# The sums of the log decays: one sequence's high and low parts stacked on the partitions, two levels at once

## What is computed

```
x_in, z = split(rmsnorm(x) @ in_proj_w)            # 512 channels each
x_in  = silu(x_in)
a_mod = sigmoid(x_in @ A_proj_w + A_proj_b)        # a decay for each token and channel
B, C  = x_in @ B_proj_w, x_in @ C_proj_w           # 16 states
for t in tokens:                                   # within one sequence
    h   = a_mod[t] * sigmoid(A_base) * h + B[t] * x_in[t]
    y[t] = sum over states of h * C[t]
out = x + ((y + D * x_in) * silu(z)) @ out_proj_w
```

## Time and profile before

| | |
|---|---|
| median of three runs | 1854.79 us |
| the runs | 1848.14, 1854.79, 1855.22 us |
| span of the profiled execution | 1852.3 us |
| busy: matmuls / weight loads | 1661.7 us / 1285.1 us |
| busy: VectorE / ScalarE / GpSimd | 1149.3 / 918.0 / 849.6 us |
| one iteration in the middle | 52.44 us |

### The profile page before, as it was taken

The page is one execution under the profiler, slowest core; times in us unless marked ns, Lnnn a source line. Parts: engine busy times, 40 slices in busy tenths (PEclk is TensorE's granted clock), DMA queues, the critical chain, the costliest instruction groups (busy, mean ns, idle before and its releaser), DMA issues.

```text
span 1852.3 us, 38642 instructions
## 1 busy us (share of the span) xinstructions
PE 1661.7 (90%) x11791; PEld 1285.1 (69%) x11791; DVE 1149.3 (62%) x2536; ACT 918.0 (50%) x2231; POOL 849.6 (46%) x552
## 2 busy tenths in 40 slices
PE   2248999999999999999999999999999999999775
PEld 2136777777777777777777777777777777777653
DVE  2465666666667666676666666666666666766432
ACT  0224555555554555555555555555545555555421
POOL 1024545555444455554444455554444555545431
PEclk9579999999999999999999999999999999999986
DMA  7110000000000000000000000000000000000000
GB/s 219 52 29 7 2 10 10 10 0 9 9 9 9 9 9 9 3 6 9 9 9 9 9 9 9 0 9 9 9 9 9 9 9 4 5 9 7 7 4 6
DMA packets 40234, 26.57 MB, mean 14 GB/s; under 512 B 19826, under 2 KB 38274, under 8 KB 40196
## 3 DMA queue, kind: packets, MB, share of 16 engines
q1 hardware_dynamic: 40196, 26.09, 5.4%
HBM read 21.37 MB, written 4.71 MB: 14 GB/s over the span
## 4 chain that ended last, share of the span: by engine, by line
PE 81%; DVE 8%; issue 5%; ACT 3%; SPq 2%; POOL 1%; DVEq 0%; DMA 0%; POOLq 0%; ACTq 0%
PE bank L742 13%; PE bank L679 13%; PE bank L707 7%; PE bank L819 6%; PE bank L633 6%; PE bank L635 5%; PE bank L634 5%; PE bank L734 4%; PE bank L720 4%; PE bank L808 3%; PE bank L834 3%; PE bank L663 2%; DVE a_sum L1264 2%; SPq L455 2%; PE bank L799 1%
## 5 line engine op out<-in xcount | busy, mean ns | idle before, releaser
L1624 POOL TENSOR_TENSOR y<-y,u 128x512 f32<-128x512 f32 x128 | 162.7, 1271 | 47.3 <-DVE u L1357 42.1
L1604 POOL TENSOR_TENSOR resid<-xres,a_c 128x256 f32<-128x256 f32 x32 | 23.3, 727 | 346.5 <-DVE x L1365 346.5
L1616 POOL TENSOR_TENSOR u<-xe,Ef 128x512 f32<-128x512 f32 x96 | 122.7, 1292 | 42.8 <-ACT Ef L1092 42.8
L679 PEld LDWEIGHTS bank<-a_xnT,a_wq 128*128 128x128 f32 x1024 | 126.8, 195 | 17.1 <-issue 14.1
L819 PE MATMUL bank<-u,Gm 128*128 128x512 f32 x256 | 130.1, 611 | 4.7 <-DVE Gm L1349 3.8
L633 PE MATMUL bank<-w_e_hi,cT_hi 128*128 128x512 f32 x256 | 122.5, 478 | 10.2 <-DVE c_c L1413 10.2
L679 PE MATMUL bank<-a_xnT,a_wq 128*128 128x128 f32 x1024 | 127.5, 279 | 0.0
L742 PEld LDWEIGHTS bank<-a_wo,a_prob 128*128 128x128 f32 x512 | 96.0, 192 | 43.9 <-ACT a_prob L995 31.8
L1585 POOL TENSOR_TENSOR a_prob<-a_prob,a_mask 128x1024 f32<-128x1024 f32 x32 | 75.6, 2363 | 109.0 <-DVE a_prob L1235 109.0
L679 PE MATMUL bank<-c_xnT,c_wq 128*128 128x128 f32 x1024 | 125.4, 282 | 0.0
L742 PE MATMUL bank<-a_wo,a_prob 128*128 128x256 f32 x512 | 120.0, 388 | 5.4 <-ACT a_prob L995 3.4
(11 more groups left out here) (294 smaller groups left out, 4427.5 us busy)
## 6 DMA issues: line engine op xcount, KB each, us to landing
a_xin<-in_x SPq DMA_DIRECT2D x32, 128.0 KB, 2.4
xres<-in_x SPq DMA_DIRECT2D x32, 128.0 KB, 2.6
out<-acc SPq DMA_DIRECT2D x32, 128.0 KB, 1.7
a_wq<-in_L_cond_Wq SPq DMA_DIRECT2D x1, 1024.0 KB, 5.4
a_wo<-in_L_cond_Wo SPq DMA_DIRECT2D x1, 1024.0 KB, 6.5
c_wq<-in_L_cond_Wq SPq DMA_DIRECT2D x1, 1024.0 KB
c_wo<-in_L_cond_Wout SPq DMA_DIRECT2D x1, 1024.0 KB
u<-in_L_ffn_expert_w SPq DMA_DIRECT2D x3, 256.0 KB, 4.0
```

The costliest lines, as they stand in the source:

```text
L679: mm = pe.matmul(bank(f"q{half}")[:, m * P:(m + 1) * P], X.wq[:, k, hp * P:(hp + 1) * P], X.xnT[:, k, :], start=k == 0, stop=k == KD - 1)
L1616: pool.tensor_tensor(u[l][:, :], xi[:, :], (E0u if l == 0 else Ef[l])[:, :], ALU.mult)\
L1624: pool.tensor_tensor(y[:, :], y[:, :], tm[l][:, :], ALU.add).then_inc(g.done(f"y{l}"), 1)
```

## The change

For each of the two sequences there is now one operand, `nl_stacked[b]` (named `nl_seq0` and `nl_seq1` in the rows), that has the high parts of the sequence's 64 tokens on one half of the partitions and the low parts on the other half. The matrix of two levels stands side by side in one 128x128 operand, its 64x64 block repeated for the two halves: one matmul sums high and low part over the contraction and gives two levels of one sequence, the first on partitions 0 to 63 of the bank, the second on 64 to 127. The four matmuls are E0 and E1 (levels 0 and 1, sequences 0 and 1) and E2 and E3 (levels 2 and 3).

- `log_a` writes the two high halves in two instructions of 64x512, waits for the second, and then takes the full logarithm as before. `nh` subtracts in two instructions of 64x512, each from one half of the partitions to the other.
- The exponentials come from banks that hold two levels of one sequence. Each is now 64x512, ten a tile in place of five. The step E0u is gone from `ORDER`; its two halves stand in E0 and E1. E0 and E1 have three exponentials each, E2 and E3 two each. Those whose level and sequence differ in number read one half of the partitions and write the other.
- The banks are freed by the last exponential that reads them. VectorE's and GpSimd's readers of a level wait for its second half.
- The table of sums and the buffer for it are half as wide.

```diff
@@ constants
-    parts["sums"] = np.concatenate(sums, 1)
+    stacked = [np.tile(a[0:S, 0:S], (2, 1)) for a in sums]
+    parts["sums"] = np.concatenate(stacked, 1)
@@ RESULTS
-"nl": "nh nl"
+"nl": "nh0 nh1 nl", "E0": "E0u0 E00 E10", "E1": "E0u1 E01 E11", "E2": "E20 E30", "E3": "E21 E31"
-"nh": "nl"
+"nh": "nl0 nl1"
@@ TURNS (which result frees the bank)
-b.E0@2>act.E0u   b.E1@2>act.E1    b.E2@2>act.E2    b.E3@2>act.E3
+b.E0@2>act.E10   b.E1@2>act.E11   b.E2@2>act.E30   b.E3@2>act.E31
@@ buffers
-        nl_parts = parts("nl", [P, E2])
+        nl_stacked = [sb(f"nl_seq{b}", [P, E2], F32R) for b in range(BT)]
@@ TensorE
-                def E(l):
+                def E(n):
+                    pair, b = n // BT, n % BT
+
                     def run(t):
-                        pe.wait_ge(*banks.free(f"b.E{l}", t))
-                        if l == 0:
-                            pe.wait_ge(*dve.at("nl", t))
-                        for n, part in enumerate(nl_parts):
-                            mm = pe.matmul(banks[f"b.E{l}"][:, :], sums[:, l * P:(l + 1) * P], part[:, :],
-                                           start=n == 0, stop=n == 1)
-                        mm.then_inc(p.done(f"E{l}"), 1)
+                        pe.wait_ge(*banks.free(f"b.E{n}", t))
+                        if n == 0:
+                            pe.wait_ge(*dve.at("nl1", t))
+                        pe.matmul(banks[f"b.E{n}"][:, :], sums[:, pair * P:(pair + 1) * P], nl_stacked[b][:, :],
+                                  start=True, stop=True).then_inc(p.done(f"E{n}"), 1)
@@ ScalarE
-                    act.activation(nl_parts[0][:, :], ae[:, :], ACT.Ln).then_inc(a.done("nh"), 1)
+                    for b in range(BT):
+                        seq = slice(b * S, (b + 1) * S)
+                        act.activation(nl_stacked[b][seq, :], ae[seq, :], ACT.Ln).then_inc(a.done(f"nh{b}"), 1)
+                    act.wait_ge(*a.at("nh1", t))
                     act.activation(nl[:, :], ae[:, :], ACT.Ln).then_inc(a.done("nl"), 1)
...
-                def E0u_(t):
-                    act.wait_ge(*p.at("E0", t))
-                    act.wait_ge(*pool.at("y0", t - 1))
-                    act.activation(E0u[:, :], banks["b.E0"][:, :], ACT.Exp).then_inc(a.done("E0u"), 1)
-
-                def E(l):
-                    def run(t):
-                        act.wait_ge(*p.at(f"E{l}", t))
-                        act.wait_ge(*dve.at(f"t{l}", t - 1))
-                        if l:
-                            act.wait_ge(*pool.at(f"u{l}", t - 1))
-                        act.activation(Ef[l][:, :], banks[f"b.E{l}"][:, :], ACT.Exp, scale=-1.0)\
-                           .then_inc(a.done(f"E{l}"), 1)
+                def E(n):
+                    pair, b = n // BT, n % BT
+                    seq = slice(b * S, (b + 1) * S)
+
+                    def run(t):
+                        act.wait_ge(*p.at(f"E{n}", t))
+                        if n == 0:
+                            act.wait_ge(*pool.at("y0", t - 1))
+                        for i in range(2):
+                            l = 2 * pair + i
+                            src = banks[f"b.E{n}"][i * S:(i + 1) * S, :]
+                            if l == 0:
+                                act.activation(E0u[seq, :], src, ACT.Exp).then_inc(a.done(f"E0u{b}"), 1)
+                            if b == 0:
+                                act.wait_ge(*dve.at(f"t{l}", t - 1))
+                                if l:
+                                    act.wait_ge(*pool.at(f"u{l}", t - 1))
+                            act.activation(Ef[l][seq, :], src, ACT.Exp, scale=-1.0).then_inc(a.done(f"E{l}{b}"), 1)
@@ VectorE
-                    dve.tensor_tensor(nl_parts[1][:, :], nl[:, :], nl_parts[0][:, :].bitcast(F32), ALU.subtract)\
-                       .then_inc(d.done("nl"), 1)
+                    for b in range(BT):
+                        seq, other = slice(b * S, (b + 1) * S), slice((1 - b) * S, (2 - b) * S)
+                        dve.tensor_tensor(nl_stacked[b][other, :], nl[seq, :], nl_stacked[b][seq, :].bitcast(F32),
+                                          ALU.subtract).then_inc(d.done(f"nl{b}"), 1)
@@ GpSimd
-                        pool.wait_ge(*act.at("E0u" if l == 0 else f"E{l}", t))
+                        pool.wait_ge(*act.at("E0u1" if l == 0 else f"E{l}{BT - 1}", t))
```

More of the change, by code:

```diff
@@ L115 @@
         c.q0@3 c.oT@4 a.expm@1 c.q1@3 a.prob@1 b.ae0@2 b.ae1@2 b.nl@2 c.qr@3 a.PT0@1 a.xnT@0 a.PT1@1
-        b.BT@2 b.E0@2 b.E0u@2 a.O0@1 a.O1@1 c.expm@3 b.E1@2 b.E2@2 c.prob@3 b.E3@2""",
+        b.BT@2 b.E0@2 a.O0@1 a.O1@1 c.expm@3 b.E1@2 b.E2@2 c.prob@3 b.E3@2""",
     "dve": """
@@ L144 @@
     1: """
-        a.q0@1>act.q0 c.ex0@4>dve.ac1 a.S1@1>dve.S1 c.ex1@4>dve.ac3 b.E2@2>act.E2""",
+        a.q0@1>act.q0 c.ex0@4>dve.ac1 a.S1@1>dve.S1 c.ex1@4>dve.ac3 b.E2@2>act.E30""",
     2: """
@@ L150 @@
         a.kv@1>dve.V b.z@2>dve.zi c.q0@3>act.q0 c.kT@3>dve.K1 c.qs@3>dve.qs a.PT0@1>act.PT0
-        b.E1@2>act.E1 b.m0@2>dve.t0""",
+        b.E1@2>act.E11 b.m0@2>dve.t0""",
     4: """
@@ L157 @@
     6: """
-        c.O1@4>act.O11 b.x@2>dve.xi c.qt@3>act.qr_l b.gt@2>act.CD3 b.E3@2>act.E3""",
+        c.O1@4>act.O11 b.x@2>dve.xi c.qt@3>act.qr_l b.gt@2>act.CD3 b.E3@2>act.E31""",
     7: """
         c.ex3@5>dve.ac7 b.m3@3>dve.t3 b.xt@2>dve.yl c.lg@4>dve.lb c.q1@3>act.q1 b.a1@2>dve.Ct
-        b.E0@2>act.E0u c.ex2@4>dve.ac5""",
+        b.E0@2>act.E10 c.ex2@4>dve.ac5""",
 }
@@ L284, in build @@
         consts = sb("consts", [P, n_consts])
-        sums = sb("sums", [P, NLV * P], F32R)
+        sums = sb("sums", [P, NLV * S], F32R)
         def const(name, rows=P):
@@ L425, in build @@
         qsq = C.OT
-        sums_staged = nl
+        sums_staged = nl[:, 0:NLV * S]
         w_in_staged = [[xe[:, :], ze[:, :]], [u[1][:, :], u[2][:, :]]]
@@ L514, in load_weights @@
                 load(sp, ld_const, consts[:, :], consts_dram[:, 0:n_consts])
-                load(sp, ld_const, sums_staged[:, :], consts_dram[:, n_consts:])
+                load(sp, ld_const, sums_staged, consts_dram[:, n_consts:])
                 sp.dma_start(A.xin[:, :], xt_dram[0]).then_inc(x_loaded.sem, 16)
@@ L1101, in scan @@
                 return {"rms": rms, "xnT": xnT, "xe": exp_x, "ze": exp_z, "xs": sig_x, "zs": sig_z, "xiT": xiT_,
-                        "ae0": exp_a(0), "ae1": exp_a(1), "nl": log_a, "BT": BT_, "E0u": E0u_, "yT": yT_}\
+                        "ae0": exp_a(0), "ae1": exp_a(1), "nl": log_a, "BT": BT_, "yT": yT_}\
                     | {f"E{l}": E(l) for l in range(NLV)}
@@ L1355, in run @@
                         dve.wait_ge(*p.at(f"m{l}", t))
-                        dve.wait_ge(*act.at(f"E{l}", t))
+                        dve.wait_ge(*act.at(f"E{l}{BT - 1}", t))
                         dve.tensor_tensor(tm[l][:, :], banks[f"b.m{l}"][:, :], Ef[l][:, :], ALU.mult)\
@@ L1467, in setup_a @@
                 setup_weights(A, prep_a, float(DH) ** -0.5)
-                dve.tensor_copy(sums[:, :], sums_staged[:, :]).then_inc(prep_a, 1)
+                dve.tensor_copy(sums[:, :], sums_staged).then_inc(prep_a, 1)
                 dve.wait_ge(prep_a, 1)
```

## The result

| | before | changed |
|---|---|---|
| median | 1854.72 us | 1906.48 us |
| the runs | 1848.14 to 1855.22 us | 1905.93 to 1906.72 us |
| span of the profiled execution | 1852.3 us | 1904.7 us |
| one iteration in the middle | 52.44 us | 54.14 us |

The ratio is 1.0292, with a 95% interval of 1.0273 to 1.0311. The direction was as forecast; the size (+26 of a forecast 1881, range 1860 to 1900) was not.

A forecast was written before the change was run, and what follows sets the result against it. ScalarE was taken to set line 742, with TensorE arriving within 0.1 us. Term 2, 0.86 us including Term 1, over 30 iterations plus about 0.5 for each end iteration gave +27 on 1854.8: 1881, range 1860 to 1900.

The forecast's parts named there:

- TensorE's saving is worth nothing: Ahead of line 742: four matmuls fewer save 0.92 us an iteration, worth nothing while ScalarE sets that line.
- TensorE is the bound: Rival, chance 0.08: ScalarE does not really hold line 742, so the 29 us of matmuls come whole: 1825.
- Half the rows, the full price: ScalarE's exponentials: one of 64x512 keeps the 128x512 pace, 0.50 us a start.
- The rival at 1847: Rival, chance 0.10: half-size exponentials at 0.25 us a start bring line 742 0.25 us earlier, 8 us in all.
- Term 1: ScalarE ahead of line 995: three exponentials instead of two make line 742 start later, +0.50 us an iteration.
- just in time: TensorE's transposes at 968.43 need a bank emptied by stream c's first score product, expected at 968.4.
- The subtraction itself: VectorE's low-part subtraction, split in two: GpSimd holds only the first half, the second costs 0.65 us more.
- Term 2: Stream c's chain from scores to transposes: the transposes come late, +0.86 us an iteration in all, Term 1 included.
- I find nothing later: Work behind stream c's transposes keeps its distance to them; nothing there becomes late.
- the wait of the transposes for the normalization: Sign that the forecast is right: stream c's transposes show a named wait on GpSimd's normalization, about 0.4 us.
- The sum: Whole kernel: 30 iterations at 0.86 us give 25.8 us, with the first and last iterations together +27.
- worse: Rival, chance 0.08: exponentials at 0.67 us a start, +1.7 an iteration, 1906; or a second subtraction of 1.43 us.

The follow-up runs named there:

- hi_only: The kernel before without its four matmuls on the low parts (result then incomplete): 1857.1 us, ratio 1.0027.
- fit2_hi_only: eight_fit2 without its four matmuls on the low parts (result then incomplete): 1817.7 us, ratio 0.9817.
- ex2_bank5: Changed kernel with the third expert product in bank 5 instead of bank 7: 1905.8 us, ratio 1.0289.
- prob_norm: Changed kernel with GpSimd's normalization of stream c ahead of its third u product and ScalarE's c.prob ahead of the E2 exponentials: 1879.5 us, ratio 1.0135.
- whole_exps: Changed kernel with five exponentials of 128x512 in place of ten of 64x512 (levels and sequences then mixed): 1857.9 us, ratio 1.0027.
- norm_first: Changed kernel with GpSimd's normalization of stream c moved ahead of its third u product: 1890.1 us, ratio 1.0206.
- m0_bank2: Changed kernel with the first mix product in bank 2 instead of bank 3: 1906.8 us, ratio 1.0299.
- four_fit2: Changed kernel with queues reordered on several engines, two bank moves, and GpSimd's y product moved away from the subtractions, which stay ahead of the scores: 1833.0 us, ratio 0.9901.
- eight_fit2: The kernel before (eight matmuls, five exponentials of 128x512) with the same moves as four_fit2: 1817.0 us, ratio 0.9830.
- four_refit: Changed kernel with neighbours reordered on several engines, including VectorE's qss step brought forward and stream c's scores ahead of the subtractions: 2010.1 us, ratio 1.0865.

## Why the prediction was right in sign and short in size

- **TensorE's saving is worth nothing: right.** hi_only shows it by itself, and so, unforeseen, does fit2_hi_only in an order without TensorE waits. The rival "TensorE is the bound" (1825) falls twice, and with it the rule of the Trainium skill cited there ("Perfetto Trace Analysis", "Identifying the Most-Contended Engine") to optimize the busiest engine first. The same section's warning about matmul busy time would not have led elsewhere: by its weight loads, 69%, TensorE was still ahead of VectorE's 62%. What decided was ScalarE's way to line 742.
- **Half the rows, the full price: right.** An exponential of 64x512 takes 0.59 us, as one of 128x512 did. The rival at 1847 falls.
- **Term 1, +0.50: too small, +0.77.** The mechanism is right (ex2_bank5, prob_norm, whole_exps). The third exponential costs 0.60, not 0.50. The other 0.16 is VectorE's: the scores start 2.32 us after the `qss` transpose instead of 1.48, so the bank of the second pair of transposes is late, which the prediction called "just in time". The weight queue shows that wait:

```profile
PEld bank L722 <- DVE c_prob L1249: 6.1, 24, 0.3
```

  The prediction added 0.65 for the subtraction and nothing for the longer logarithm. The halves cost 0.61. They started 0.11 later after VectorE's `qss` than the subtraction did, since the logarithm ended only at 988.49, 0.21 us ahead of them, so the 0.2 us that the prediction saw to spare there was not enough. A last 0.11 comes at their end: `Bt` starts 0.03 after it, where it started 0.08 ahead of the subtraction's; why is open.
- **The subtraction itself: right, and for the stated reason.** Two halves of 2.04 against the predicted 2.08; 1.40 without the product beside them.
- **Term 2, +0.86: the step that failed.** Its path was right; a hold on it was put at nothing. Predicted positions against measured ones, from the `qss` transpose: `c_prob` 12.84 and 13.13, the sum 14.00 and 14.21, the normalization 15.88 and 16.72, the transposes 17.93 and 18.68. Up to the sum the chain is 0.2 us off. Then the prediction took 1.88 us from the sum's start to the normalization's from the kernel before; it took 2.51, and the 0.63 between is `c_den`. The prediction had even worked out that GpSimd's third `u` product would now end just as the normalization was to start, and took it for a second path of nearly equal length. It did not ask what VectorE would do beside it. The rule it had cited for the subtraction (the Trainium skill, "SBUF — State Buffer", "Who interferes with whom") covers this case: `c_den` has two SBUF inputs, the product reads SBUF, and the product came first. The trace agrees, 0.80 us with and 0.18 without. norm_first puts 16 us on it, GpSimd's queue included. Of the 0.84 us that an iteration is longer than forecast, 0.21 are there when the sum starts and 0.63 are `c_den`.
- **"I find nothing later": wrong as a statement, harmless in time.** Line 657 waits 0.55 us for a bank behind `c_den`; m0_bank2 shows that the transposes pay the same. That is why the wait of the transposes for the normalization, which the prediction named as a sign, did not show: line 657 waited in front of them.
- **The sum.** 0.86 x 30 = 26 became 1.70 x 30 = 51: 1.61 at the transposes, and 0.09 behind them that was not followed up. The rival "worse" came out at its number, 1906, by another mechanism than its two: exponentials at 0.57 a start, not 0.67, and a subtraction of 2.04, not 2.86.

Whether the loss belongs to the change or to the order around it: of the 52 us, prob_norm gives back 27 by order alone, and four_fit2 more than all. But eight_fit2 gains more from the same moves, so in the orders tried the change itself costs 16 us or more.

## What to carry to other kernels

TensorE's busy share of 90% and more did not tell what a saving on it was worth: nothing, in two orders. Look for the wait that ends last, and for who pays for the saving (here 128 matmuls against 160 exponentials and 64 smaller instructions). When a change moves instructions of VectorE or GpSimd in time, lay the two engines' rows over each other again at the new times: a short VectorE instruction on a chain can cost what is left of the long GpSimd product that it falls beside, here 0.80 us for 0.18. A named wait is a place to look, not a price: take it away and see whether the next one in line takes its time.

## What the hardware did that was not expected

- In these rows VectorE was held for about the rest of GpSimd's instruction whatever its own size: `c_den`, 128x16, took 0.63 us more, and a 64x512 subtraction that takes 0.69 alone took 2.7. Two kinds were not held: a sum over 128x1024 (in the kernel before it starts 0.32 us into a `u` product and takes 1.21, no more than alone) and instructions that read a bank. In four_fit2, beside one normalization on GpSimd (1003.49 to 1005.46), `qss` from a bank kept its 0.29 while the next instruction, from SBUF, took 1.67 instead of 0.41:

```profile
1003.73 0.29 DVE L1235 TENSOR_SCALAR qss<-bank 128x128 f32<-128x128 f32 x1
1003.93 1.67 DVE L1201 TENSOR_SCALAR a_xn<-a_xin,a_mv,a_rstd 128x256 f32<-128x256 f32 x1
```

  It went the other way too. In eight_fit2 VectorE's subtraction of the maximum (1.23 us alone) was held by the `u` product that began at 1003.93 and ended at 1005.20; the next product, beside the rest of the subtraction, then took 2.25 us instead of 1.27:

```profile
1004.06 2.22 DVE L1258 TENSOR_TENSOR c_prob<-c_prob,c_mx 128x1024 f32<-128x1024 f32 x1
```

```profile
1003.93 1.27 POOL L1616 TENSOR_TENSOR u<-xe,u 128x512 f32<-128x512 f32 x1
1005.16 2.25 POOL L1616 TENSOR_TENSOR u<-xe,Ef 128x512 f32<-128x512 f32 x1
```

- In four_refit TensorE's granted clock fell after it had waited, which made the loss larger than the waits. Windows of that kernel (columns of the earlier trace rows); in the second the granted clock is 0.53, near the lower level of 1.2 GHz, after a stretch with a wait of 2.04 us:

```profile
980.77:985.05 4.28, 2.00 (x15) 1.36 (x13) 3.03 (x5) 2.65 (x9) 1.69 (x1) 0.90 0.00 0
985.05:995.00 9.95, 8.21 (x23) 4.51 (x24) 7.42 (x7) 8.47 (x18) 5.87 (x4) 0.53 0.00 0
995.00:1005.00 10.00, 9.86 (x63) 7.23 (x65) 7.16 (x16) 4.12 (x11) 6.34 (x6) 1.00 0.00 0
```

  The wait, and the eight matmuls of line 736 in the stretch behind it:

```profile
983.47 0.44 PE L649 MATMUL bank<-consts,a_xn 128*128 128x128 f32 x2 [2.04 <-DVE Bt L1355]
...
985.35 1.98 PE L736 MATMUL bank<-a_qT,a_V 64*64 64x512 f32 x8
```

  The changed kernel, at a granted clock of 1.00, has them in 1.09:

```profile
993.31 1.09 PE L736 MATMUL bank<-a_qT,a_V 64*64 64x512 f32 x8
```
